# First columns of the scan inputs set aside, router weights on another engine, and a different first chunk in a two-layer kernel with a selective scan

## The reference, cut to what matters

```python
x, gate = split(h @ W_in.T)                      # 1024 channels each
xc = conv_b + sum(conv_w[:, j] * xpad[:, j:j+L]) # 4 taps, causal
x = silu(xc)
ts, B, C = split(rms(x @ W_x.T))                 # 32, 16, 16 columns
dt = softplus(ts @ W_dt.T + b_dt)
state = state * exp(dt * A) + (dt * x) * B       # 16 states per channel, over time
y = (sum(state * C) + x * D) * silu(gate)
x1 = x0 + ga * (y @ W_out.T)
logits = h @ router_W.T                          # 8 experts
w = top-2 of softmax(logits), normalised to 1
out = x1 + gb * (h @ base_W.T + ((h @ lora_A) * w) @ lora_B * 2)
```

## Time and profile before

| What | Value |
|---|---|
| Median of 3 runs | 1589.07 us |
| The profiled execution | 1589.25 us, span 1587.5 us |
| TensorE, VectorE busy in the span | 1393.3 us (88%), 1252.2 us (79%) |
| GpSimd, ScalarE busy in the span | 1079.0 us (68%), 911.9 us (57%) |
| Layer 1's scan: first and last scan start | 542.9 and 1549.8 us |
| 512 scans of VectorE | 626.9 us |
| 256 scan inputs of GpSimd | 604.3 us |
| Mean granted clock of TensorE | 0.952 of full |

### The profile page before, as it was taken

The page is one execution under the profiler, slowest core; times in us unless marked ns, Lnnn a source line. Parts: engine busy times, 40 slices in busy tenths (PEclk is TensorE's granted clock), DMA queues, the critical chain, the costliest instruction groups (busy, mean ns, idle before and its releaser), DMA issues.

```text
span 1587.5 us, 25291 instructions
## 1 busy us (share of the span) xinstructions
PE 1393.3 (88%) x8809; PEld 999.4 (63%) x8809; DVE 1252.2 (79%) x1677; ACT 911.9 (57%) x2416; POOL 1079.0 (68%) x957
## 2 busy tenths in 40 slices
PE   6699999999999679699799799889889989978677
PEld 5467677766776467467557557657656756755543
DVE  5684674556333389989999999999999999999993
ACT  3333342324222676767777777686687687775641
POOL 0353233322323498898998998999899899899970
PEclk9699999999999889699999999999999999999678
DMA  9431321200000200300210110110030030020001
GB/s 332 165 110 35 107 81 54 80 27 14 28 27 33 67 1 1 94 1 2 69 39 1 55 53 1 46 62 1 8 100 1 1 107 1 1 68 27 1 1 40
DMA packets 32389, 77.17 MB, mean 49 GB/s; under 512 B 3667, under 2 KB 4723, under 8 KB 31750
## 3 DMA queue, kind: packets, MB, share of 16 engines
q1 hardware_dynamic: 32262, 75.55, 14.2%
HBM read 66.99 MB, written 8.55 MB: 48 GB/s over the span
## 4 chain that ended last, share of the span: by engine, by line
POOL 24%; PE 16%; DVE 14%; issue 7%; ACT 6%; DVEq 0%; POOLq 0%; ACTq 0%
POOL dbu L1921 13%; DVE h L2093 9%; POOL h L1943 6%; DVE acc L2106 4%; PE ps_o L1447 4%; PE ps_h L1423 3%; ACT ps_a L1633 2%; PE ps_h L1411 1%; PE ps_m L1386 1%; POOL dbu L1925 1%; PE ps_m L159 1%; PE ps_m L161 1%; PE ps_m L160 1%; POOL dtu L2024 1%; POOL dt L1988 1%
## 5 line engine op out<-in xcount | busy, mean ns | idle before, releaser
L2093 DVE TENSOR_TENSOR_SCAN h<-ps_a,carry,dbu 128x512 f32<-128x512 f32 x512 | 626.9, 1266 | 18.4 <-ACT carry L1646 6.7
L1921 POOL TENSOR_TENSOR dbu<-dtu,b_all 128x1024 f32<-128x1024 f32 x256 | 604.3, 2361 | 29.4 <-DVE h L2093 16.8
L1633 ACT ACTIVATE ps_a<-dt,a_neg 128x256 f32<-128x256 f32 (+1 forms) x1024 | 443.7, 467 | 151.3 <-DVE h L2093 150.8
L1423 PE MATMUL ps_h<-ident,h 128*128 128x128 f32 x1536 | 232.6, 295 | 104.0 <-DVE acc L2106 89.6
L1423 PEld LDWEIGHTS ps_h<-ident,h 128*128 128x128 f32 x1536 | 187.4, 152 | 158.8 <-DVE h L2093 113.0
L2106 DVE SCALAR_TENSOR_TENSOR acc<-ps_h,c_cur,acc 128x512 f32<-128x512 f32 x384 | 267.9, 738 | 8.6 <-PE ps_h L1423 8.2
L708 POOL TENSOR_TENSOR hid_l<-hid,hid_h 128x256 f16<-128x256 f32 (+1 forms) x88 | 77.5, 884 | 156.7 <-ACT hid_h L599 156.6
L1943 POOL TENSOR_TENSOR h<-h,c_all 128x1024 f32<-128x1024 f32 x64 | 150.9, 2358 | 13.4 <-ACT carry L1646 13.4
L591 ACT ACTIVATE sil<-ps_gu 128x256 f32<-128x256 f32 (+1 forms) x88 | 34.0, 386 | 180.9 <-PE ps_gu L161 180.9
L159 PE MATMUL ps_m<-h_h,wi_h 128*128 128x256 f16 x440 | 121.7, 277 | 5.9 <-PEq L149 2.4
L160 PE MATMUL ps_m<-h_l,wi_h 128*128 128x256 f16 x440 | 121.0, 275 | 0.0
(11 more groups left out here) (349 smaller groups left out, 2849.4 us busy)
## 6 DMA issues: line engine op xcount, KB each, us to landing
b_all<-bt_scratch SPq DMA_DIRECT2D x32, 512.0 KB, 4.2
wm<-in_wmod SPq DMA_DIRECT2D x7, 1024.0 KB, 5.0
wo<-in_wmod SPq DMA_DIRECT2D x5, 1024.0 KB, 7.1
xa<-in_x SPq DMA_DIRECT2D x8, 512.0 KB, 4.2
stage<-in_W_in SPq DMA_DIRECT2D x4, 1024.0 KB
x_scratch<-x SPq DMA_DIRECT2D x8, 512.0 KB, 3.2
c_all<-bt_scratch SPq DMA_DIRECT2D x8, 512.0 KB, 6.3
x<-x_scratch SPq DMA_DIRECT2D x8, 512.0 KB, 3.6
```

The source lines that it names most:

```text
L1423: tr = pe.transpose(ps_h[:, t, j * P:(j + 1) * P], h[:, s % RING, j, t * P:(t + 1) * P], W["ident"][:])
L1633: ex = nc.scalar.activation(ps_a[:, j, j % 2:], dt[:, m, j % 2:], ACT.Exp, scale=a_neg[:, m, st:st + 1])
L1921: nc.gpsimd.tensor_tensor(dbu[:, s % AHEAD], dtu[:], b_all[:, st, :].unsqueeze(1).to_broadcast([P, DG, CH]), ALU.mult).then_inc(S["db_mul" ...
L2093: nc.vector.tensor_tensor_scan(h[:, s % RING, two].rearrange("p j t -> p (j t)"), ps_a[:, two].rearrange("p j t -> p (j t)"), dbu[:, s % A ...
```

## The change

It has three parts.

1. **Scan inputs' first columns.** GpSimd's product now leaves out column 0 of each tile, and the add behind it is gone. For a whole group of 16 steps at once GpSimd computes the first columns in `fold` (`first_inputs`: dtu's column 0 times B's column 0 for all steps, then the products of decay and old state, made by `old_state`, added to the odd tiles). ScalarE copies them into `dbu`, two steps in one instruction, ahead of the exps of every even step (`heads`). B's column 0 is needed on all partitions: TensorE spreads it with one more matmul in `turn_tsb`, ScalarE copies it to `b0`. For group 0 of chunk 0 the old state is zero and is left out.
2. **Router weights on VectorE.** `gap_of` and GpSimd's `weigh` go. ScalarE takes exp(-a + b) straight from the two largest logits (two instructions, step 20). VectorE does the rest in eight instructions in step 22, behind `rms_apply`, with a reciprocal in place of a power.
3. **First chunk.** Five PSUM banks in place of three. The convolutions of tiles 1, 3, 5 and 7 are done by VectorE from `xw` into `u`, the other four by TensorE. Wx is issued tile by tile behind each `u`. VectorE's and GpSimd's diagonals are made in another order; VectorE makes those of tiles 1 and 3, which chunk 1 needs first, between the tiles.

```diff
@@ first chunk
+        if first:
+            return (ps_m[:, 0], ps_m[:, 1], ps_s, ps_h[:, 0], ps_h[:, 1])[m % 5][:, 0:CH]
         return ps_m[:, m % 3, 0:CH] if m % 3 < 2 else ps_s[:, 0:CH]
...
+        def wx_first(k):
+            pe.wait_ge(S["u_done"], k + 1)
+            mm = pe.matmul(wx_bank(True), W["wx"][:, k], u[:, k, :], start=(k == 0), stop=(k == KI - 1))
...
-        for m in range(KI):
-            if m > 2:
-                convolve(0, m - 2, True)
-            x_tile(0, m, True)
-            if m == 2:
-                convolve(0, 0, True)
-        convolve(0, KI - 2, True)
-        convolve(0, KI - 1, True)
-        wx(0)
+        for m in range(3):
+            x_tile(0, m, True)
+        convolve(0, 0, True)
+        x_tile(0, 3, True)
+        x_tile(0, 4, True)
+        convolve(0, 2, True)
+        wx_first(0)
+        x_tile(0, 5, True)
+        convolve(0, 4, True)
+        wx_first(1)
+        x_tile(0, 6, True)
+        wx_first(2)
+        x_tile(0, 7, True)
+        wx_first(3)
+        convolve(0, 6, True)
+        for k in range(DG, KI):
+            wx_first(k)
...
+        def convolve_first(m):
+            dve.wait_ge(S["xw_done"], 3 * m + 3)
+            done = MADE_CONV[m] - TAPS
+            nc.vector.tensor_scalar(u[:, m], xw[:, 1, 0:CH], taps[:, m, 0:1], taps[:, m, TAPS:TAPS + 1], ALU.mult, ALU.add)\
+              .then_inc(S["made"], 1)
+            for tap in range(1, TAPS):
+                dve.wait_ge(S["made"], done + tap)
+                nc.vector.scalar_tensor_tensor(u[:, m], xw[:, 1, tap:tap + CH], taps[:, m, tap:tap + 1], u[:, m], ALU.mult, ALU.add)\
+                  .then_inc(S["made"], 1)
...
-        for m in range(KI):
+        for m in range(0, KI, 2):
+            convolve_first(m + 1)
             make_u(0, m, True)
+            make_u(0, m + 1, True)
+            if m < DG:
+                diagonals(m + 1)
@@ turn_tsb, tsb_in
+            pe.matmul(ps_s[:, CH:CH + NS], W["ident"][:, 0:1].to_broadcast([P, P]), ssn[:, 0, RDT:RDT + NS], start=True, stop=True)\
+                .then_inc(S["tsb_mm"], 1)
...
+            nc.scalar.activation(b0[:], ps_s[:, CH:CH + NS], ACT.Copy).then_inc(S["b0_done"], 1)
@@ ScalarE, at the head of exps for even s
+        def heads(i, s):
+            act.wait_ge(S["fold_done"], (i * 2 + s // NS + 1) * 3)
+            if i or s >= AHEAD:
+                act.wait_ge(S["scan_half"], i * (2 * STEPS) + 2 * (s - AHEAD + 2))
+            nc.scalar.activation(dbu[:, s % AHEAD:s % AHEAD + 2, :, 0], fold[:, s:s + 2, :], ACT.Copy)
@@ router_exp, step RA_AT + 3 (was RA_AT + 5)
-            act.wait_ge(S["gap_done"], p + 1)
-            nc.scalar.activation(e2[:], gap[:], ACT.Exp).then_inc(S["e2_done"], 1)
+            act.wait_ge(S["top_done"], p * TT + TT)
+            for t in range(TT):
+                op = nc.scalar.activation(e2[:, t:t + 1], top[:, t, 0:1], ACT.Exp, scale=-1.0, bias=top[:, t, 1:2])
+            op.then_inc(S["e2_done"], 1)
@@ GpSimd
-            nc.gpsimd.tensor_tensor(dbu[:, s % AHEAD], dtu[:],
-                                    b_all[:, st, :].unsqueeze(1).to_broadcast([P, DG, CH]), ALU.mult).then_inc(S["db_mul"], 1)
-            pool.wait_ge(S["db_mul"], value(i, STEPS, s))
-            head = dbu[:, s % AHEAD].rearrange("p (a b) t -> p a b t", b=2)[:, :, 1, 0]
-            nc.gpsimd.tensor_tensor(head, head, fold[:, s, :], ALU.add).then_inc(S["dbu_done"], 1)
+            nc.gpsimd.tensor_tensor(dbu[:, s % AHEAD, :, 1:], dtu[:, :, 1:],
+                                    b_all[:, st, 1:].unsqueeze(1).to_broadcast([P, DG, CH - 1]), ALU.mult).then_inc(S["dbu_done"], 1)
...
+        def first_inputs(n, g):
+            pool.wait_ge(S["dtu_done"], n * 2 + (g + 1))
+            pool.wait_ge(S["b0_done"], n + 1)
+            pool.sem_inc(W["met_pool"], 1)
+            steps = slice(g * NS, (g + 1) * NS)
+            op = nc.gpsimd.tensor_tensor(fold[:, steps, :], dtu[:, :, 0].unsqueeze(1).to_broadcast([P, NS, DG]),
+                                         b0[:].unsqueeze(2).to_broadcast([P, NS, DG]), ALU.mult)
+            if n == 0 and g == 0:
+                op.then_inc(S["fold_done"], 3)
+                return
+            op.then_inc(S["fold_done"], 1)
+            pool.wait_ge(S["fold_done"], (n * 2 + g) * 3 + 2)
+            odd = fold[:, steps, :].rearrange("p n (a b) -> p b n a", b=2)[:, 1]
+            nc.gpsimd.tensor_tensor(odd, odd, decay0[:, g * 2:g * 2 + 2, :].rearrange("p a n -> p n a"), ALU.add)\
+              .then_inc(S["fold_done"], 1)
...
-        for m in range(DG, KI):
+        for m in (4, 6, 5, 7):
@@ VectorE, step RA_AT + 5
+        def weigh(p):
+            dve.wait_ge(S["top_at_done"], p * TT + TT)
+            nc.vector.tensor_copy(at[:], top_at[:, :, 0:2]).then_inc(S["weigh_step"], 1)
+            dve.wait_ge(S["e2_done"], p + 1)
+            nc.vector.tensor_scalar(e2p[:], e2[:], 1.0, None, ALU.add).then_inc(S["weigh_step"], 1)
+            dve.wait_ge(S["weigh_step"], p * 7 + 1)
+            nc.vector.tensor_tensor(wd[:], expert[:]..., at[:]..., ALU.is_equal).then_inc(S["weigh_step"], 1)
+            dve.wait_ge(S["weigh_step"], p * 7 + 2)
+            nc.vector.reciprocal(w12[:, :, 0], e2p[:]).then_inc(S["weigh_step"], 1)
+            dve.wait_ge(S["weigh_step"], p * 7 + 4)
+            nc.vector.tensor_tensor(w12[:, :, 1], w12[:, :, 0], e2[:], ALU.mult).then_inc(S["weigh_step"], 1)
+            dve.wait_ge(S["weigh_step"], p * 7 + 5)
+            nc.vector.tensor_tensor(wd[:], wd[:], w12[:]..., ALU.mult).then_inc(S["weigh_step"], 1)
+            dve.wait_ge(S["weigh_step"], p * 7 + 6)
+            nc.vector.tensor_tensor(wd[:, 0], wd[:, 0], wd[:, 1], ALU.add).then_inc(S["weigh_step"], 1)
+            dve.wait_ge(S["weigh_step"], p * 7 + 7)
             nc.vector.tensor_tensor(mid..., rl[:, :, NE:]..., wd[:, 0]..., ALU.mult).then_inc(S["mid_done"], 1)
```

More of the change, by code:

```diff
@@ L1205, in gate_bank, with wx_bank @@
         return ps_m[:, m % 2, 0:CH]
-    wx_bank = ps_m[0:RDT + 2 * NS, 1, 0:CH]
+    def wx_bank(first):
+        return (ps_o if first else ps_m[:, 1])[0:RDT + 2 * NS, 0:CH]
     def t3_bank(t):
@@ L1317, in x_tile @@
                 pe.wait_ge(S["t3_lo"], n * TT)
-            if m < 2:
-                if not first:
-                    pe.wait_ge(S["gate_sg"], (n - 1) * KI + (KI - 1 + m))
+            if first:
+                if m in (2, 7):
+                    take_s(S["u_done"], m + 1)
+                elif m > 4:
+                    pe.wait_ge(S["u_done"], m - 4)
+            elif m < 2:
+                pe.wait_ge(S["gate_sg"], (n - 1) * KI + (KI - 1 + m))
             else:
@@ L1326, in x_tile @@
             cols = slice(m * P, (m + 1) * P)
-            products(pe, x_bank(m), [(W["wi_h"][:, k, cols], W["wi_l"][:, k, cols]) for k in range(KD)], h3)\
+            products(pe, x_bank(m, first), [(W["wi_h"][:, k, cols], W["wi_l"][:, k, cols]) for k in range(KD)], h3)\
                 .then_inc(S["x_mm"], 1)
@@ L1383, in convolve @@
             if first:
[L1384 removed]
+                pe.wait_ge(*((S["made"], MADE_DIAG[m]) if m < DG else (S["diag_more"], ((m - DG) // 2 + 1) * TAPS)))
+            elif n == 1 and m == 1:
+                pe.wait_ge(S["made"], MADE_DIAG[3])
+                pe.wait_ge(S["diag_more"], DG * TAPS)
             for tap in range(TAPS):
[L1386 to L1387 removed]
+                pe.matmul(x_bank(m, first), diag_t[:, m, tap], xw[:, m % 2, tap:tap + CH], start=(tap == 0), stop=False)
+            pe.matmul(x_bank(m, first), W["cb"][:, m * P:(m + 1) * P], W["ones"][32:34, :], start=False, stop=True)\
                 .then_inc(S["conv_pe"], 1)
@@ L1698, in x_tanh @@
                 act.wait_ge(S["gate_sg"], n * KI + (m - 1))
-            nc.scalar.activation(th[:, m % 2], x_bank(m), ACT.Tanh).then_inc(S["tanh_done"], 1)
+            nc.scalar.activation(th[:, m % 2], u[:, m] if first and on_dve(m) else x_bank(m, first), ACT.Tanh).then_inc(S["tanh_done"], 1)
         def gate_tanh(i, m, first=False):
@@ L1853, in others @@
                     nc.scalar.preload_act_table_set("exp_and_others")
-            if p is not None and s == RA_AT + 5:
+            if p is not None and s == RA_AT + 3:
                 router_exp(p)
@@ L2033, in others @@
                 inv_std_b(p)
-            if p is not None and s == RA_AT + 6:
-                gap_of(p)
-            if p is not None and s == RA_AT + 9:
-                weigh(p)
             if s == 12:
-                fold_carry(i, 1, first)
+                old_state(i, 1)
             if s == NS - 1:
                 dt_u(i, 1)
+                first_inputs(i, 1)
             if n is not None and s == STEPS - 3:
@@ L2119, in make_u, with diagonals @@
                 dve.wait_ge(S["dtu_done"], n * 2)
-            nc.vector.scalar_tensor_tensor(u[:, m], th[:, m % 2], 1.0, x_bank(m), ALU.add, ALU.mult).then_inc(S["u_done"], 1)
```

(21 more changed lines are left out.)

115 lines of the change are left out of this document (47 added, 68 removed).

## The result

The changed kernel takes 1621.83 us (median of 4 runs, 1620.92 to 1624.51), the kernel before 1588.49 in the same comparison: ratio 1.0211, 95% interval 1.0193 to 1.0229. The forecast was 1584.7 us with a range to 1593. The time is outside it, on the other side of the old one, and 37 us from the forecast.

What follows compares the result with a forecast made beforehand. VectorE and GpSimd were both almost full; the change was priced by where VectorE idles. Terms -9.3 - 1.5 - 1.1 - 1.5 - 0.8 + 9.6 = -4.6 us gave 1584.7 us, with 1576 to 1593 to hold 8 in 10.

Steps and rivals of the forecast that it cites:

- 3. Router weights on VectorE: Step 22 of each chunk: eight small VectorE operations cost 1.6 us, in full in chunks 1 to 6, +9.6 us.
- The prediction's own sign of being wrong: Period of chunks 2 to 6: growth of 2 us or more, against about 1.3 expected, would mean copies or weights dearer.
- the +9.6 of the sum: Total cost in us forecast for the router weights on VectorE, over chunks 1 to 6.
- another rule, on fixed cycles: VectorE's router weights: 58 fixed cycles per operation plus columns give 0.84 us; about 150 measured cycles give 1.61 us.
- 1. First chunk: Layer 1 before the first scan: input, convolution and Wx end after 22.4 us, gain 9.3 us, bounds 8 and 9.6.
- 2. Scan inputs' first columns: GpSimd loses 11 us of work per chunk; gains of 1.5, 1.1, 1.5 and 0.8 us, ScalarE's copies free.
- The rival that made them dear: ScalarE's 128 copies delay the exps by 0.12 us each, 15 us in all, 1600 us; chance 0.12.
- GpSimd as the bound: Rival for chunks 2 to 6: GpSimd causes VectorE's idles; 1571 us, with half of that 1578; chance 0.15.
- fall into the 2.58 us: Last chunk: the router weights fit into VectorE's wait behind TensorE, of which 1.8 us are left; cost zero.
- the chance of 0.10 for slower: Probability given to the changed kernel being slower than before by over 0.3%.

Runs made afterwards that it cites:

- experiment 3: The changed kernel with one added wait: GpSimd holds the scan input of step 24 until VectorE has finished that chunk's router weights; 1586.58 us, ratio 0.9982.
- experiment 7: The kernel before with only the first-chunk part of the change added; 1582.94 us, ratio 0.996.
- experiment 2: The changed kernel with the router weights left on GpSimd as in the kernel before; 1576.66 us, ratio 0.9906.
- experiments 4 and 5: The kernel before with small two-column VectorE probe operations added per chunk, seven, then four at steps where some had waited; 1632.41 and 1603.51 us, one run each.

## Why the prediction was wrong, point by point

**The step that failed is "3. Router weights on VectorE": 1.6 us per chunk, "bounds 1.1 to 2.4".** It should have been some 6.8. In the trace, the five periods between chunk 2 and chunk 7 take 662.86 us with the weights on VectorE and 628.82 with them on GpSimd: 6.8 each. The prediction's own sign of being wrong came up with it: the period grew by 6.3 us from before, where 2 was the mark. Of the 6.8, 6.15 are the eight operations and the rest small idles and accumulates behind them. By the medians, each against the kernel before of its own comparison, part 2 is worth 33.3 + 13.7 = 47 us, against the +9.6 of the sum.

Why the price came out so: I took it from the earlier trace rows, where GpSimd has nothing to do any more, and from two MAX8 in the earlier trace rows, which have a single SBUF input. Both are true, and experiment 3 measures 1.47 us once GpSimd stands still. What I didn't ask is whether the row's surroundings were those of the place to which the work goes. At that place GpSimd is busy 94 of 100 us, and from the first scan on every VectorE instruction beside it in the kernel before has a PSUM operand or a single tensor input (scan, accumulate, gate, the ssn products, MAX8). So no row of layer 1 shows the wait. (The search behind MAX8 names two SBUF tiles and took 0.16 us there.) But the trace of before does show it, in layer 0, which the change leaves alone and of which the prediction uses no row. VectorE's scalar_tensor_tensor on 512 columns with two SBUF inputs, beside GpSimd and right after it alone:

```profile
95.33 2.36 POOL L691 TENSOR_TENSOR d_l<-wi_h,d_h 128x1024 f16<-128x1024 f32 x1
```
```profile
95.73 2.51 DVE L807 SCALAR_TENSOR_TENSOR msum<-wm,silu_c,msum 128x512 f32<-128x512 f32 x1
...
98.28 0.75 DVE L807 SCALAR_TENSOR_TENSOR msum<-wm,silu_c,msum 128x512 f32<-128x512 f32 x1
```

The first ends at 98.24, 0.55 us behind GpSimd's end at 97.69: it waited, and then did its own work. An operation of a few columns has hardly any work of its own left, and so seems to end with GpSimd's. The rows of layer 0 would have priced the move at the length of the neighbour's instruction, 2.37 us, as the upper bound for each operation with two SBUF inputs. With five such operations, the copy and the addition that is up to 7 x 2.37 = 16.6 us per chunk; 6.3 was measured, since GpSimd runs out of work after three scan inputs. That nobody is held would have been the other end, 1.6.

**A rule that was left out.** The Trainium skill, "GPSIMD Engine Reference", sections "Specifications" and "Key points", states that GpSimd shares its SBUF interfaces with VectorE, in contention with VectorE instructions "in a 2-port perf mode or with two SBUF inputs". The traces agree: the scalar_tensor_tensor and the product with two inputs wait beside GpSimd (1.64 and 1.75 us), reciprocal and reduction don't (0.12 to 0.14). The copy and the tensor_scalar have one input and wait too (1.37 to 1.55); that they ran in a 2-port mode fits, but no trace shows the mode. These two sections give no price; the runs do: a short operation ends when the running GpSimd instruction ends. The prediction weighed another rule, on fixed cycles.

**"1. First chunk": right in mechanism.** -8.4 us to the reading of Wx's result, forecast -9.3. TensorE has its four groups of eight, Wx follows tile by tile. Not all of it was kept in the changed kernel. TensorE in order of time, then the busy time of the stretch:

```profile
518.10 2.08 PE L1380 MATMUL ps_o<-u,wx 128*64 128x256 f32 x8
...
526.46 5.64 PE L1369 MATMUL ps_m<-tsb,w_dt 128*128 128x256 f32 x16 [1.62 <-issue]
```
```profile
525.00:530.00 5.00, 3.54 (x9) 2.77 (x10) 0.26 (x2) 2.68 (x6) 0.00 (x0) 0.69 0.27 90
```

The missing microsecond is mostly Wx in pieces: each of the four portions of two matmuls takes TensorE 0.57 us and the last one of eight 2.1, together 4.4, where 3.67 us had been counted for all sixteen. VectorE's convolutions took 2.0 to 2.2 us, not 1.7 (three scalar_tensor_tensors in 1.53 to 1.63), but the last u was there at 519.4, before the last of these eight needed it: TensorE sets the end. Then the dt tiles ran at a granted clock of 0.69, 5.64 us. In experiment 7, at 1.00, they ended 4.4 us after their start, and there all of the 8.3 us reached the first scan (40.34 us from the first product, 41.60 in the changed kernel). Experiment 3, which has part 1 as well, shows the same 40.34 at a clock of 1.00, so part 1 gives nothing back here.

**"2. Scan inputs' first columns": right.** Chunk 0's first part -2.4 us instead of -1.5; the wait for rms fell from 1.3 to 0.2 us (forecast -1.1); the periods by 0.5 us instead of 0.3. ScalarE's copies between 540 and 1586 us, to be held against the earlier trace rows:

```profile
L1675 ACT ACTIVATE dbu<-fold 128x8 f32<-128x8 f32 x127 | 26.5, 209 | 0.0
```

0.209 us each, priced at 0.207 and hidden. The rival that made them dear (1600, 0.12) was wrong, and so was GpSimd as the bound: experiment 2 is at 1576.7, about where that rival stood (1578), but the period fell by 0.5 us, not by 1.4 and more.

**The last chunk's weights "fall into the 2.58 us": wrong** for the same reason, 6.3 us don't fit into 1.8; it costs one more period's worth.

Without step 3 my own sum is -14.2 us, and experiment 2 measured -13.7. That they meet is partly luck. In experiment 2's trace only 5.3 us of the forecast 9.3 reach the first scan (48.69 to 43.35 us from the first product): Wx's result came 1.7 us later than in the changed kernel and the dt tiles took 5.7 us instead of 4.4, with two falls of the granted clock in that stretch. Behind the first scan it gained 4.6 us up to chunk 2, 2.8 in the five periods and 2.0 behind them, 9.4 in place of the forecast 4.9. The one slower rival was about ScalarE's copies, and the chance of 0.10 for slower went with it; the dearest term of the sum had no rival beyond its 2.4 us.

## What to carry to other kernels

Before an operation is moved to VectorE beside a busy GpSimd, look at its form: with two SBUF inputs, or as a copy or tensor_scalar, count for it the rest of the GpSimd instruction that is running on top of its own work, and do so for each one in a chain. A long operation of this kind on VectorE holds GpSimd's next instruction in turn. A price is to be read from a row whose neighbour engines do what they will do at the new place. Look for such rows in every stage of the trace, also in those that the change leaves alone: here layer 0 had them. Such a wait shows as busy time: a group whose mean is ten times that of its like is the sign, and the list of waits stays empty.

## What the runs showed of the hardware

- A VectorE operation on 2 to 32 columns takes 0.12 to 0.19 us alone and, with two SBUF inputs or as a copy or tensor_scalar, up to 2.34 us beside GpSimd's elementwise instructions of 2.35 us. GpSimd isn't slowed by operations this short (2356 ns a scan input with the weights on VectorE, 2355 without).
- Long operations with two SBUF inputs hold GpSimd too. In layer 0 of the kernel before, GpSimd's product of 0.68 us took 2.35 when it began 0.6 us behind a VectorE operation on 2048 columns, and ended 0.5 us after it. VectorE's row and GpSimd's:

```profile
211.49 2.43 DVE L849 SCALAR_TENSOR_TENSOR bsum<-stage,shift,bsum 128x2048 f32<-128x2048 f32 x1
```
```profile
212.10 2.35 POOL L708 TENSOR_TENSOR hid_l<-hid,hid_h 128x256 f16<-128x256 f32 x1 [0.33 <-ACT hid_h L599]
...
215.08 0.68 POOL L708 TENSOR_TENSOR hid_l<-hid,hid_h 128x256 f16<-128x256 f32 x1 [0.64 <-ACT hid_h L599]
```

- An added wait of an engine that isn't the bound can free another: 35 us in experiment 3, of which 1.3 lie ahead of the first scan and go with the granted clock there.
- Between two long GpSimd instructions back to back a constant addition slips through (0.15 us at 1020.14 in the changed kernel), and the next operation with two SBUF inputs meets the following one in full (2.28 us). A reciprocal wasn't held at any of its places in experiments 4 and 5.
